# Two cross-attention layers: the order in which maximum pieces and score chunks alternate on TensorE, and heads written out instead of looped

## What is computed

```python
    def _L1_xattn_ref(query, value, wq, bq, wk, bk, wv, bv, wo, bo):
        ...
        scores = jnp.einsum('bhqd,bhkd->bhqk', q, k) / scale
        attn = jax.nn.softmax(scores, axis=-1)
        ctx = jnp.einsum('bhqk,bhkd->bhqd', attn, v)
        ctx = ctx.transpose(0, 2, 1, 3).reshape(B, -1, D_MODEL)
        return ctx @ wo.T + bo
```

## Time and profile before

| what | value |
|---|---|
| median of 3 runs | 1890.03 us (1886.89 to 1894.4) |
| profiled execution, its own time | 1891.61 us |
| its span in the trace | 1889.9 us |
| PE busy | 1545.9 us (82%) |
| DVE busy | 1178.3 us (62%) |
| ACT busy | 861.1 us (46%) |
| mean granted clock of TensorE | 0.901 of full |

### The profile page before, as it was taken

How to read it: one execution, slowest core, us unless ns; L and a number is a source line. 1 busy time by engine, 2 the same in 40 slices (tenths; PEclk the granted TensorE clock), 3 DMA queues, 4 the chain that set the end, 5 groups by cost and what they waited for, 6 DMA issues and landing times. The chain is left out here.

```text
span 1889.9 us, 27747 instructions
## 1 busy us (share of the span) xinstructions
PE 1545.9 (82%) x7833; PEld 910.5 (48%) x7834; DVE 1178.3 (62%) x2309; ACT 861.1 (46%) x1544; POOL 182.0 (10%) x248
## 2 busy tenths in 40 slices
PE   6464999968997999992399999999999998657880
PEld 3132443347785788882154444444444434544550
DVE  2564988763211677766398888888898853622334
ACT  3021767722112555541127777676776775221110
POOL 3520000000300000003000000000000000061106
PEclk9786999987999999996659999999999999788995
DMA  7935312111102899971722121111211100424114
GB/s 242 373 116 156 102 43 51 27 46 67 45 1 88 300 348 336 335 250 48 212 67 67 42 44 23 22 22 30 35 22 22 22 1 1 113 89 129 38 50 133
DMA packets 108654, 196.61 MB, mean 104 GB/s; under 512 B 8958, under 2 KB 80371, under 8 KB 108567
## 3 DMA queue, kind: packets, MB, share of 16 engines
q1 hardware_dynamic: 101633, 180.71, 30.9%
q0 software_dynamic: 4608, 12.59, 2.1%
q10 hardware_dynamic: 2326, 2.31, 0.4%
HBM read 144.69 MB, written 50.36 MB: 103 GB/s over the span
## 5 line engine op out<-in xcount | busy, mean ns | idle before, releaser
L910 DVE TENSOR_REDUCE attend_piece_max<-attend_p_bank 128x1 f32<-128x400 f32 (+3 forms) x1280 | 671.8, 588 | 108.1 <-PE attend_p_bank L798 90.7
L890 ACT ACTIVATE attend_probs<-attend_s_bank 128x512 f32<-128x512 f32 (+1 forms) x1088 | 565.3, 602 | 284.4 <-PE attend_s_bank L809 284.2
L798 PE MATMUL attend_p_bank<-attend_k_st,attend_q_st 62*128 62x400 f32 (+2 forms) x1280 | 412.3, 418 | 62.8 <-DMA attend_k_st<-ones_rows 52.3
L809 PE MATMUL attend_s_bank<-attend_q_st,attend_k_st 64*128 64x512 f32 (+1 forms) x1088 | 385.5, 461 | 26.8 <-ACT attend_probs L890 13.6
L809 PEld LDWEIGHTS attend_s_bank<-attend_q_st,attend_k_st 64*128 64x128 f32 (+1 forms) x1088 | 170.9, 185 | 348.9 <-ACT attend_probs L890 338.0
L826 PE MATMUL attend_o_bank<-attend_probs,attend_v_st 128*32 128x512 f32 (+1 forms) x2176 | 293.4, 611 | 1.4 <-ACT attend_probs L890 1.4
L798 PEld LDWEIGHTS attend_p_bank<-attend_k_st,attend_q_st 62*128 62x128 f32 x1280 | 223.1, 198 | 109.5 <-issue 54.0
L1520 DVE TENSOR_TENSOR slots_w_low<-slots_w_up,slots_w_high 128x2048 fp32r<-128x2048 f32 x46 | 105.1, 2287 | 46.9 <-ACT slots_w_high L1516 46.9
L1330 DVE TENSOR_TENSOR share_hid<-share_b_bank,share_g_act 128x512 f32<-128x512 f32 (+1 forms) x40 | 27.6, 691 | 120.5 <-PE share_b_bank L1181 89.8
L1516 ACT ACTIVATE slots_w_high<-slots_w_up 128x2048 fp32r<-128x2048 f32 x46 | 87.8, 1910 | 6.8 <-DMA slots_w_up<-in_L_ffn_W_dram 6.6
L1787 POOL DMA_INDIRECT collect_back<-back,keep_f_place x48 | 47.0, 980 | 386.4 <-PEq L1776 372.4
(11 more groups left out here) (234 smaller groups left out, 1811.0 us busy)
## 6 DMA issues: line engine op xcount, KB each, us to landing
slots_w_up<-in_L_ffn_W_dram SPq DMA_DIRECT2D x46, 1024.0 KB, 7.9
slots_w_dn<-in_L_ffn_W_dram SPq DMA_DIRECT2D x23, 1024.0 KB, 6.1
ctx_raw<-in_mask_BxSxS_ik_dram SPq DMA_DIRECT2D x16, 800.5 KB, 8.1
q_rows<-q_part SPq DMA_DIRECT2D x24, 512.0 KB, 4.3
attend_q_st<-q_rows SPq DMA_DIRECT2D x64, 192.0 KB, 4.6
k_rows<-ctx_k_part SPq DMA_DIRECT2D x12, 800.5 KB, 10.5
attend_k_st<-k_rows SPq DMA_DIRECT2D x32, 300.2 KB, 6.1
sorted<-keep_zeros SPq DMA_DIRECT2D x6, 1024.0 KB, 8.5
```

What stands on the lines that cost most here:

```text
L798: last = pe.matmul(bank[:, 0:even(kn)], q_st[rows, slot, t * P:(t + 1) * P].bitcast(F32R), k_st[rows, slot, k0:k0 + even(kn)].bitcast(F32R ...
L809: last = pe.matmul(out, k_st[rows, hs, kt * P:kt * P + kn].bitcast(F32R), q_st[rows, hs, q0:q0 + CH].bitcast(F32R), start=True, stop=not m ...
L890: act.activation(probs[0:kn, (kt + hs) % RING, q0:q0 + CH], s_bank[(NC * kt + c + hs) % RING][0:kn, :], ACT.Exp).then_inc(exp_done, 1)
L910: dve.tensor_reduce(dst, bank_of(i, n)[:, 0:kn], AX.X, ALU.max).then_inc(entry_done, 1)
```

## The change

Three things change.

1. `side_by_side` reorders a step's pieces: the first of them is of half 1, and from there the halves alternate as long as both have pieces. In layer 1 a step with pieces 4 to 8 goes 5, 4, 7, 6, 8, and one with 9 to 13 stays 9, 10, 11, 12, 13. In layer 0 each step goes 1, 0, 3, 2. "maxima" is inserted afterwards, still at index 2. Which piece is meant by a number, and the banks, which follow from the place in the order, stay.
2. The tuple in PE's body has chunk 0, one piece, chunk 1, one piece, chunk 2, one piece, product, chunk 3, the rest; before it had chunks 0 and 1 and then two pieces.
3. Passes 4 to 15 are written out as straight code on all engines in layer 1 and in layer 0's window branch. Layer 0's other branch, which does not run with these inputs, keeps the loop.

```diff
@@ class Keys
-    def __init__(self, first, size, pieces, late, maxima_at):
+    def __init__(self, first, size, pieces, late, maxima_at, looped=False):
+        self.looped = looped
@@ attend
+        def side_by_side(now):
+
+            halves, taken = [now[1::2], now[0::2]] if now and now[0] % 2 == 0 else [now[0::2], now[1::2]], []
+            for k in range(len(now)):
+                taken.append((halves[k % 2] or halves[1 - k % 2]).pop(0))
+            return taken
...
             for s in range(KT):
-                now = list(range(cuts[s], cuts[s + 1])) if mx else []
+                now = side_by_side(list(range(cuts[s], cuts[s + 1]))) if mx else []
...
-            for i in range(4):
+            for i in range(4 if keys.looped else H):
                 once(i)
-            with eng.Fori(4, H - RING + 1, RING) as j:
-                for u in range(RING):
-                    body(j + u, (4 + u) % RING, True, True, True)
+            if keys.looped:
+                with eng.Fori(4, H - RING + 1, RING) as j:
+                    for u in range(RING):
+                        body(j + u, (4 + u) % RING, True, True, True)
...
-            with sp.Fori(4, H - RING, RING) as j:
-                for u in range(RING):
-                    body(j + u, (4 + u) % RING, True, True, True)
-            for i in range(H - RING, H + 1):
+            if keys.looped:
+                with sp.Fori(4, H - RING, RING) as j:
+                    for u in range(RING):
+                        body(j + u, (4 + u) % RING, True, True, True)
+            for i in range(H - RING if keys.looped else 4, H + 1):
                 body(i, i % RING, True, True, True)
...
-                    for chunks, first, end in (((0, 1), 0, 2), ((2,), 2, 3), ((3,), 3, None)):
+                    for chunks, first, end in (((0,), 0, 1), ((1,), 1, 2), ((2,), 2, 3), ((3,), 3, None)):
@@ flamingo_kernel
-        everything = Keys(0, S, PIECES, 4, (1, 2))
+        everything = Keys(0, S, PIECES, 4, (1, 2), looped=True)
+        unmasked = Keys(0, S, PIECES, 4, (1, 2))
...
-                    attend(nc, const, scratch, l, everything, attn, row_max)
+                    attend(nc, const, scratch, l, unmasked, attn, row_max)
```

## The result

The changed kernel takes 1841.33 us in the median of 4 runs (1838.9 to 1846.52), the one before 1888.85 us over 4 (1886.89 to 1894.4). The ratio is 0.974, with a 95% interval of 0.970 to 0.978: 47.5 us less. The forecast was 1846, with a range of 1830 to 1868. Of the experiments' runs, two of the kernel that is only written out and two of the kernel before had a mean granted clock of 0.88 and took over 1.5% longer than the fastest; medians and ratios leave these four out.

The account below looks back on a forecast made before the run. A ring through PE and ACT (product, chunk 3, chunk 2, product) was taken to set layer 1's steps, with loops costing separately. Terms 14.1 + 2.6 + 19.5 + 8.4 + 1.2 = 45.8 off 1891.6 gave 1846 us, range 1830 to 1868.

Parts of the forecast that it names:

- Heads written out: Passes 2 to 15: without the loops' jumps and register work, 14.1 us less in layer 1 and 2.6 in layer 0.
- the 5.6 us kept as a bound: Layer 1: part of the gain lost if all straight passes were like pass 3 (37.55) and not pass 2 (37.15).
- New order, layer 1: Layer 1 steps: piece and chunk 2 run side by side on two halves; 1.39 us a pass, 19.5 in all.
- DVE's pause of 0.70: Layer 1, each second step: DVE pauses 0.70 us where the first piece behind the product is of half 1.
- New order, layer 0: Layer 0: DVE's pauses of 0.36 and 0.45 go, 0.21 is lost after "maxima"; 0.60 a pass, 8.4 us.
- Passes 1: The passes 1, which have a part of the steps, add 1.2 us (eight at 0.15).
- Sum: Whole kernel: 14.1 + 2.6 + 19.5 + 8.4 + 1.2 = 45.8 us less than the profiled 1891.6.
- (a): Layer 1: the order brings nothing, as DVE still lets pieces go late; gain 25, 1866 us; chance 0.14.
- (b): Both layers: the order brings nothing anywhere, only the loops count; gain 16.7, 1875 us; chance 0.07.
- (c): Straight code: a 2.90 us stop in each pass, as engines have more code to fetch; 1876 us; chance 0.05.
- (d): Layer 1: the special steps shrink too, the pass nears 34.5, 18 us more gain; 1828 us; chance 0.1.
- (e): PE's queue: a piece waiting for its bank holds up chunk 1 and ACT behind it; +91 - 46, 1935 us; chance 0.02.

Follow-up runs that it names:

- the mended kernel: Changed kernel, but in the step with "maxima" the pieces behind the turn begin with half 0; 1842.91 us, and 1851.82 when run again, ratio 0.973 both times.
- the kernel with the third piece behind: Changed kernel, but nothing stands between chunk 2 and the product, the third piece being issued behind chunk 3; 1909.29 us, ratio 1.011 to the kernel before.
- the kernel with the wrong halves: Changed kernel, but each step's pieces begin with half 0, so the third piece shares chunk 2's half; 1880.88 us, ratio 0.994 to the kernel before.

## Why the prediction was right

**Heads written out, 14.1 + 2.6.** Measured alone 14.2 + 2.6. Taking straight pass 2 and not pass 3 as the model was right; the 5.6 us kept as a bound did not arise, as pass 3's 0.4 comes with the loop behind it.

**New order, layer 1, 19.5.** Measured 18.5 (520.01 to 501.55), 1.32 a pass and not 1.39. The mechanism is the one forecast: DVE begins 0.15 earlier in the late steps, the step is 2.60, and swapping halves the other way makes it 2.79. Step by step, five gained 0.92 in all (0.95 in the sum), five 0.55 (0.60), and the one behind the maxima lost 0.15 (0.16); mending it gave back 0.16 a pass. One row was read too widely: DVE's pause of 0.70 was taken for that of each second step, and it stands in one step of a pass only, 0.44 in the others. The sum did not use it.

**New order, layer 0, 8.4.** Measured 8.0, 0.57 a pass for 0.60. The total is nearer than its terms, which is in part luck. Of DVE's two pauses the 0.36 went, but of the second, 0.46 in straight code, 0.19 is left: the text had said that 0.4 of it would go, and the sum took all 0.45. What made up for it is DVE's busy time, which fell from 11.13 to 10.97 and had no term: a reduction that follows another without a pause adds 0.60, one alone takes 0.69. The loss behind the maxima was 0.20 (0.21 in the sum), and the mended kernel gave it back.

**Passes 1, 1.2.** In the changed kernel's layer 1 pass 1 took 34.61, in the one before 36.01; in layer 0 10.76 and 11.00: 1.6. Layer 0's part of it is no measurement: in the second profile of the changed kernel that pass took 11.60.

**Sum, 45.8.** The touched passes gave 44.9 (43.2 and 1.6). The medians differ by 47.5; the rest is within the scatter outside. The profiled execution of the changed kernel, 1838.9, is 7 us under the forecast; the stretch between the layers, for which no change had been forecast, took 7.6 us less.

**Rivals.** (a) and (b) are out: the piece starts 0.01 behind chunk 2. The row that spoke for (a), a piece 0.17 late though its half is free, was DVE's late start, as argued: 1.71 behind the product, and 1.56 now. (c) is out: no stop in passes 4 to 15. (d) did not arise, the step with "sums" is still 3.75 and the one with "maxima" 2.80 (2.82). (e) shows only in the kernel with the third piece behind.

**A step that was not seen.** The prediction added the two parts as if each were worth the same with and without the other. It came out right because the order's term was worked out for straight code. In the loop it would have been 1.00 a pass and not 1.39.

## What to carry to other kernels

When a chain through several engines sets a step, look for the instruction that stands between two links of it, and ask what it shares with its neighbours: here it was half of the array's rows, worth 0.11 to 0.19 us a step, while pairing at places where nothing waits was worth nothing. A stretch of the same kernel that leaves that instruction out is the best estimate of what the chain costs without it. Where code of one stage is changed, compare that stage pass by pass; the passes showed a gain of 4.9 us here that the whole time hid on one chip and showed in part, 3.3, on the next, since the rest of the program scatters by more.

## What was not expected of the hardware

A jump back over a loop body of three layer 1 passes costs 3.5 to 5.8 us (40.79 and 41.94 against 37.33 before, 42.08 against 36.33 with the new order). DVE stands 2.90 us for nothing that the profile names (2.79 with the new order), and the granted clock of the pass falls to 0.96, 0.92 and 0.88, from 2.4 GHz to 1.2 GHz for a part of it. The same loop in layer 0, whose passes are about a third as long, showed no such stop, only 0.4 at most: its fourteen passes lost 2.6 us in all, 0.1 to 0.2 at a jump. What decides between the two was not tried.

Two matmuls of different halves start 0.01 us apart and run together; two of the same half start 0.34 apart where the first streams 512 columns after loading its weights. A matmul can also start ahead of others that stand before it in the program. Of the kernel with the wrong halves, behind the product of 1136.09:

```profile
1137.08 0.51 PE L822 MATMUL attend_s_bank<-attend_q_st,attend_k_st 64*128 64x512 f32 x2
1137.42 0.53 PE L811 MATMUL attend_p_bank<-attend_k_st,attend_q_st 62*128 62x402 f32 x3
```

The two chunks are chunk 3 of half 1 and chunk 0 of half 0. In the program at least one piece of half 1 stands between them, and no piece starts before 1137.42.

The outside of the passes, the same code in all kernels but for the pieces of passes 0 and 1, ranged from 1167.9 to 1192.2 us over twelve profiled executions, with mean granted clocks of 0.87 to 0.89 between the layers and 0.78 to 0.84 behind them. Behind them the longest stretches on the first chips had the lowest clocks: 370.71 at 0.78 and 361.17 at 0.81, against 349.3 to 352.7 at 0.83 and 0.84. On the last chip 359 to 363 went with 0.82 to 0.84, so the clock is not all of it, and why it differs stays open.
